# Draining a weight-preparation queue four times as fast inside attention, with its first rounding step moved from VectorE to ScalarE

## The chip, the cores and the metric

The kernel runs on all 8 cores of one Trainium2 chip. Each core takes two of the sixteen sequences (2048 tokens of width 1024) and prepares the FFN weights for itself; the cores do not talk to one another. The time is that of the slowest core, in microseconds (us) of device time. The engines are PE (TensorE), DVE (VectorE), ACT (ScalarE), POOL (GpSimd) and SP (SyncE, here an issuer of transfers). Each has its own instruction stream in program order; semaphores couple them.

## The reference, cut to what matters

Per sequence: attention whose softmax runs over the queries (axis -2), a residual and a layer norm; then an FFN with quantized weights and activations, a depthwise convolution over three tokens, another residual and layer norm.

```python
q, k, v = x @ Wq.T + bq, x @ Wk.T + bk, x @ Wv.T + bv
scores = where(j > i, -inf, q @ k.T / 32)          # [2048, 2048] per sequence
x = layernorm(x + softmax(scores, axis=-2) @ v)

def weight_quant(w):                               # w1: [4096, 1024], w2: [1024, 4096]
    scale = 1.0 / clip(mean(abs(w)), 1e-5)
    return clip(round(w * scale), -1, 1) / scale
h = act_quant(x) @ weight_quant(w1).T
h = silu(depthwise_conv1d(h, conv_w, conv_b))      # 3 taps along the tokens
x = layernorm(x + act_quant(h) @ weight_quant(w2).T)
```

## The kernel before, in words

The program is written as one list of operations (`Prog.op`). Each names its engine and the tiles it reads and writes, and the builder turns dependences into semaphore waits. Within an engine the order is the order of the list. A transfer is issued by the engine that it is listed on, and that engine's stream stands still until the waits of the transfer are met. Transfers on ACT are dealt in turn to four streams (`n_act_dma % 4`), and each also waits for the one before it on its stream; SP's and POOL's wait for the previous one of their engine. A transposing transfer (`xbar=True`) waits for the last transfer of every stream, and all later transfers wait for the last transposing one.

Stages, in order:

- Start (to about 170 us): constants, and Wq, Wk, Wv cast to bf16 into scratch memory.
- `attn(b)` for b = 0 and 1. The x loop (L416 on, 16 tiles) loads x, casts it on DVE, stores it. Then transposing loads of x and Wv (in batch 0 of Wq and Wk too). The v loop (L458 on) has 32 groups of 8 matmuls, each evacuated by DVE (L470). The q and k loops (L476 on) have 32 groups each, evacuated by ACT (L491), over four PSUM banks. The score loop has 16 steps `jt`: matmuls (L521), mask and maxima on DVE (L528, L534), exponentials on ACT (L549), column sums and the scaling of v on DVE (L555 to L561). The PV loop has 16 iterations `it` of 2·(it + 1) matmuls (L578); DVE adds the two banks to x (L585), a layer norm runs over DVE, ACT and POOL, the result is quantized (L636, L640), transposed on PE (L646), copied by ACT (L650) and stored by POOL (L653, s_xqT). At the end of a batch one small store of row maxima (s_m1, L664).
- `ffn_entry()`: 8 transposing loads of the quantized W1 (L815) and 32 of W2. The first waits for all attention tiles and all weight stores.
- The FFN, 16 chunks and a tail.

The weight preparation is a queue of closures, `prep_q`, made by `build_prep_queue()`. It goes over W1 and W2 twice, each in 128 tiles of 128x256. First pass, per matrix: load a tile (`_pload`, L674, issued on ACT), sum its absolute values (`_p1c`, L680, DVE), and at the end one mean (`_pmean`). Second pass: load the tile again, then `_p2c`: three DVE steps (L718: times scale plus MAGIC, which rounds; L723: minus MAGIC, minimum with 1; L727: maximum with -1, to bf16) and a store issued on ACT (L731). Loads are listed three tiles ahead of their compute; there are four input buffers (`PR_in`) and two output buffers (`PR_ob`). The queue has 512 loads, 512 computes and 2 means, 1026 entries. `drain(n)` lists the next n entries at its place; each of the attention loops calls it once an iteration, and `while prep_q: drain(1)` lists what is left between `attn(1)` and `ffn_entry()`.

Of the kernel before, what the change touches and what calls it, by code (L numbers as in the profile page):

```python
# [9 lines left out]
AF = mybir.ActivationFunctionType  # L10
ALU = mybir.AluOpType
AX = mybir.AxisListType.X

MAGIC = 12582912.0
# [166 lines left out]
def build_program(T=2048, NB=2, debug=False):  # L181
# [3 lines left out]
    p = Prog()  # L185
# [65 lines left out]
    misc = P_("misc", [128, 64], F32)  # L251
# [21 lines left out]
    for jt in range(NT):  # L273
# [15 lines left out]
           for t in range(NT)]  # L289
# [18 lines left out]
    PR_in = [mem.at(PRS + i * 1024, f"PR_in{i}", [128, 256], F32)  # L308
             for i in range(4)]
# [44 lines left out]
         writes=["idenf"])  # L354
# [12 lines left out]
    p.op("POOL", lambda e: e.memset(neghalf[:], -0.5), writes=["neghalf"])  # L367
    p.op("POOL", lambda e: e.memset(zpad[:], 0.0), writes=["zpad"])
    p.op("POOL", lambda e: e.memset(misc[:, 60:64], 0.0), writes=["msczero"])

    for b in range(NB):
        for e8 in range(ECH):
# [42 lines left out]
    def attn(b):  # L415
        for it in range(NT):  # L416
            sl = slice(it * 128, (it + 1) * 128)
            p.op("SP", lambda e, sl=sl, it=it: e.dma_start(
                out=A_x32[it % 2][:], in_=x_d[b, sl, :]),
                writes=[f"x32_{it % 2}"], dma=True)  # L420
            p.op("DVE", lambda e, it=it: e.tensor_copy(
                out=A_xbf[it % 2][:], in_=A_x32[it % 2][:]),
                reads=[f"x32_{it % 2}"], writes=[f"xbf{it % 2}"])
            p.op("POOL", lambda e, sl=sl, it=it: e.dma_start(
                out=s_xbf[b, sl, :], in_=A_xbf[it % 2][:]),
                reads=[f"xbf{it % 2}"], writes=[f"sxbf{it}"], dma=True)
            drain(1)
        p.fence([f"xT{e}" for e in range(ECH)]
                + [f"WvT{e}" for e in range(ECH)] + ["BVbc", "bvrow"],
                [f"P{jt}" for jt in range(NT)])  # L430
# [28 lines left out]
        for it in range(NT):  # L459
            g = it % 2  # L460
            bk0, bk1 = 2 * g, 2 * g + 1
            for h, bk in ((0, bk0), (1, bk1)):
                for e8 in range(ECH):
                    p.op("PE", lambda e, it=it, h=h, bk=bk, e8=e8: e.matmul(  # L464
                        out=B[bk][:],
                        lhsT=A_xT[e8][:, it * 128:(it + 1) * 128],
                        rhs=A_WvT[e8][:, h * 512:(h + 1) * 512],
                        start=(e8 == 0), stop=(e8 == ECH - 1)),
                        reads=[f"xT{e8}", f"WvT{e8}"], writes=[f"B{bk}"])
                p.op("DVE", lambda e, it=it, h=h, bk=bk: e.tensor_tensor(  # L470
                    out=A_v[it][:, h * 512:(h + 1) * 512], in0=B[bk][:],
                    in1=A_BVbc[:, h * 512:(h + 1) * 512], op=ALU.add),
                    reads=[f"B{bk}", "BVbc"], writes=[f"v{it}"])
                drain(1)

        icw = min(512, T)  # L476
        for dstl, wTl, bc, nm in ((A_qT, A_WqT, bqc, "q"), (A_kT, A_WkT, bkc, "k")):
            wkey = "WqT" if nm == "q" else "WkT"
            for fc in range(ECH):
                for ic in range(T // icw):  # L480
                    bk = (fc * (T // icw) + ic) % 4
                    for e8 in range(ECH):
                        p.op("PE", lambda e, fc=fc, ic=ic, bk=bk, e8=e8,
                             wTl=wTl: e.matmul(  # L484
                            out=B[bk][:, 0:icw],
                            lhsT=wTl[e8][:, fc * 128:(fc + 1) * 128],
                            rhs=A_xT[e8][:, ic * icw:(ic + 1) * icw],
                            start=(e8 == 0), stop=(e8 == ECH - 1)),
                            reads=[f"xT{e8}", f"{wkey}{e8}"], writes=[f"B{bk}"])
                    p.op("ACT", lambda e, fc=fc, ic=ic, bk=bk, dstl=dstl,  # L490
                         bc=bc: e.activation(  # L491
                        out=dstl[fc][:, ic * icw:(ic + 1) * icw],
                        in_=B[bk][:, 0:icw],
                        func=AF.Identity, bias=bc[:, fc:fc + 1], scale=1.0),
                        reads=[f"B{bk}", "b" + nm + "c"],
                        writes=[f"{nm}T{fc}"])
                    drain(1)

        p.fence([f"P{jt}" for jt in range(NT)],
                [f"xT{e}" for e in range(ECH)] + [f"WvT{e}" for e in range(ECH)]  # L500
# [2 lines left out]
        for jt in range(NT):  # L503
            c0 = jt * 128
            bounds = [c0]
            nxt = (c0 // 512 + 1) * 512
            while nxt < T:
                bounds.append(nxt)
                nxt += 512
            bounds.append(T)  # L510
            chunks = [(bounds[i], bounds[i + 1] - bounds[i])
                      for i in range(len(bounds) - 1)]
            nch = len(chunks)
            banks = []
            for ci in range(nch):
                banks.append(gchunk % 6)
                gchunk += 1
            for e8 in range(ECH):
                for ci, (cs, w) in enumerate(chunks):
                    bk = banks[ci]  # L520
                    p.op("PE", lambda e, e8=e8, jt=jt, cs=cs, w=w, bk=bk: e.matmul(  # L521
                        out=B[bk][:, 0:w],
                        lhsT=A_kT[e8][:, jt * 128:(jt + 1) * 128],
                        rhs=A_qT[e8][:, cs:cs + w],
                        start=(e8 == 0), stop=(e8 == ECH - 1)),
                        reads=[f"kT{e8}", f"qT{e8}"], writes=[f"B{bk}"])
            bk0 = banks[0]
            p.op("DVE", lambda e, bk0=bk0: e.tensor_tensor(  # L528
                out=B[bk0][:, 0:128], in0=B[bk0][:, 0:128], in1=maskneg[:],
                op=ALU.add),  # L530
                reads=[f"B{bk0}", "maskneg"], writes=[f"B{bk0}"])
            for ci, (cs, w) in enumerate(chunks):
                bk = banks[ci]
                p.op("DVE", lambda e, bk=bk, w=w, ci=ci: e.tensor_reduce(  # L534
                    out=misc[:, CMAX0 + ci:CMAX0 + ci + 1], in_=B[bk][:, 0:w],
                    axis=AX, op=ALU.max),
                    reads=[f"B{bk}"], writes=[f"cmax{ci}"])
            p.op("DVE", lambda e, nch=nch: e.tensor_reduce(
                out=mc(MRAW), in_=misc[:, CMAX0:CMAX0 + nch], axis=AX,
                op=ALU.max),  # L540
                reads=[f"cmax{ci}" for ci in range(nch)], writes=["Mraw"])
            p.op("DVE", lambda e: e.tensor_scalar(
                out=mc(BIASV), in0=mc(MRAW), scalar1=-1.0 / 32.0, scalar2=None,
                op0=ALU.mult),
                reads=["Mraw"], writes=["biasv"])
            for ci, (cs, w) in enumerate(chunks):
                bk = banks[ci]
                p.op("ACT", lambda e, bk=bk, w=w, jt=jt, cs=cs, c0=c0,
                     ci=ci: e.activation(  # L549
                    out=A_P[jt][:, cs - c0:cs - c0 + w], in_=B[bk][:, 0:w],  # L550
                    func=AF.Exp, bias=mc(BIASV), scale=1.0 / 32.0,
                    accum_out=misc[:, CSUM0 + ci:CSUM0 + ci + 1]),
                    reads=[f"B{bk}", "biasv"],
                    writes=[f"P{jt}", f"csum{ci}", f"B{bk}_free"])
            p.op("DVE", lambda e, nch=nch: e.tensor_reduce(  # L555
                out=mc(COLSUM), in_=misc[:, CSUM0:CSUM0 + nch], axis=AX,
                op=ALU.add),
                reads=[f"csum{ci}" for ci in range(nch)], writes=["colsum"])
            p.op("DVE", lambda e: e.reciprocal(out=mc(RCOL), in_=mc(COLSUM)),
                 reads=["colsum"], writes=["rcol"])  # L560
            p.op("DVE", lambda e, jt=jt: e.tensor_scalar(  # L561
                out=A_v[jt][:], in0=A_v[jt][:], scalar1=mc(RCOL), scalar2=None,
                op0=ALU.mult),
                reads=["rcol", f"v{jt}"], writes=[f"v{jt}"])
            drain(2)

        p.fence(["xres", "xln0", "xln1", "xqstg", "xqbf", "pvx0", "pvx1"],
                [f"qT{e}" for e in range(ECH)])
        for it in range(NT):
# [73 lines left out]
            for e8 in range(ECH):  # L643
# [11 lines left out]
                .rearrange("e p t -> p e t"),  # L655
                in_=PV_xqstg[:].rearrange("p (e t) -> p e t", e=ECH)),
                reads=["xqstg"], writes=[f"sxq{b}_{it}"], dma=True)
            drain(3)
        p.op("PE", lambda e: e.transpose(
            out=B[5][0:NT, 0:128], in_=m1ct[:], identity=iden_f[:]),  # L660
            reads=["m1ct", "idenf"], writes=["B5"])
# [51 lines left out]
    def _p2c(g, m, sd, rows, cols, skey):  # L713
        rwbk = f"rwb{m + 1}"
        rwbc = RWB1 + m
        up = g % 4
        ob = (g // 1) % 2
        p.op("DVE", lambda e, up=up, rwbc=rwbc: e.tensor_scalar(  # L718
            out=PR_in[up][:], in0=PR_in[up][:],
            scalar1=misc[:, rwbc:rwbc + 1], scalar2=MAGIC,  # L720
            op0=ALU.mult, op1=ALU.add),
            reads=[f"pin{up}", rwbk], writes=[f"pin{up}"])
        p.op("DVE", lambda e, up=up: e.tensor_scalar(  # L723
            out=PR_in[up][:], in0=PR_in[up][:], scalar1=MAGIC, scalar2=1.0,
            op0=ALU.subtract, op1=ALU.min),
# [57 lines left out]
    def drain(n=1):  # L783
        for _ in range(n):
            if prep_q:
                prep_q.pop(0)()
# [391 lines left out]
```

How the kernel before makes its waits and increments, by code:

```python
            def section(_):  # L134
                waited = {f: 0 for f in self.ENGINES}
                for i, emit, inc, deps in ops:
                    want = {}
                    for d in deps:
                        f = openg[d]
                        v = cums[d]
                        if v > want.get(f, 0):
                            want[f] = v
                    for f, v in want.items():
                        if waited[f] < v:
                            eo.wait_ge(sems[f], v)
                            waited[f] = v
                    inst = emit(eo)
                    if inc:
                        inst.then_inc(sems[streams[i]], inc)
```

## Time and profile before

| | us |
|---|---|
| two runs | 3976.15 and 4021.40 |
| their median | 3998.77 |
| the profiled execution | 3978.36 |
| its span on the slowest core (core 3) | 3976.5 |
| spans of the eight cores | 3942.6 to 3976.5 |

| engine | busy us | share of the span |
|---|---|---|
| PE matmul | 2043.1 | 51% |
| DVE | 1608.5 | 40% |
| ACT | 1117.4 | 28% |
| POOL | 153.8 | 4% |

The table of engines is a mean over stages that have different limits. The granted clock of PE is 0.76 of full speed over the span. In the profile's forty slices of 99 us, PE is busy in slices 4 to 17 (attention, in two humps with weak stretches between), at zero in slices 18 to 22, and at seven to eight tenths from slice 24 to the end (the FFN). So a reader looks at stretches of time first, then at what releases what within one.

### The profile page before, as it was taken

The page shows a single profiled execution, that of the slowest core. Times are in us where ns is not written, and L with a number is a line of the kernel's source. Part 1 is how long each engine was busy: PE and PEld are TensorE (multiplying, and loading weights), DVE is VectorE, ACT ScalarE, POOL GpSimd, SP SyncE. Part 2 cuts the span into 40 slices and gives each one's busy share as a digit, 9 for nine tenths or more (in the row PEclk, how much of TensorE's full clock was granted, in tenths as well). Part 3 has the DMA queues.
Part 4 walks back from the last instruction along what each step waited for, and adds up shares of the span by engine and source line. Part 5 has one row for each costly group of instructions (what it writes and reads, how often), then busy time and mean ns, then how long its engine had stood idle before and what let it go on. Part 6 is the DMA issues. An engine that isn't in the chain of part 4 may idle for free.

```text
span 3976.5 us, 43318 instructions; the slowest of 8 cores (3942.6 to 3976.5 us)
## 1 busy us (share of the span) xinstructions
PE 2043.1 (51%) x10824; PEld 1129.4 (28%) x10824; DVE 1608.5 (40%) x4913; ACT 1117.4 (28%) x2978; POOL 153.8 (4%) x264
## 2 busy tenths in 40 slices
PE   0005972341398434300000387777777777787776
PEld 0002430110143111100000254444444444454442
DVE  0102134332122533356650255555555455555554
ACT  0000422220023222100000354444444444444442
POOL 2100000101000010000000000000000000000000
PEclk9998995665598756655555688787888888888877
DMA  1653103224410243355555200000000000000000
GB/s 46 206 137 69 38 19 85 76 81 130 88 38 23 59 86 70 69 148 151 147 139 114 69 17 17 28 27 27 27 27 27 27 25 24 17 27 28 17 22 22
DMA packets 298170, 248.47 MB, mean 62 GB/s; under 512 B 153858, under 2 KB 268738, under 8 KB 297924
## 3 DMA queue, kind: packets, MB, share of 16 engines
q1 hardware_dynamic: 169860, 105.05, 11.1%
q10 hardware_dynamic: 110592, 83.94, 7.7%
q0 software_dynamic: 17472, 56.72, 4.6%
q8 instruction: 92, 1.51, 0.2%
q14 instruction: 154, 1.26, 0.1%
HBM read 138.58 MB, written 73.48 MB: 53 GB/s over the span
## 4 chain that ended last, share of the span: by engine, by line
PE 37%; DMA 23%; DVE 19%; issue 9%; ACT 9%; POOL 1%; DVEq 1%; ACTq 1%; SPq 0%; POOLq 0%
PE bank L993 10%; PE bank L874 8%; PE bank L484 6%; PE bank L578 4%; DVE F_u L981 4%; PE bank L895 3%; DMA s_w2i<-PR_ob 3%; DMA s_w1i<-PR_ob 3%; DVE Fg L984 3%; DMA A_x<-x 3%; DMA F_W2qT<-s_w2i 3%; PE bank L521 3%; PE bank L464 2%; DMA A_xT<-s_xbf 2%; ACT F_D L887 2%
## 5 line engine op out<-in xcount | busy, mean ns | idle before, releaser
L874 PE MATMUL bank<-F_xq,F_W1qT 128*128 128x258 bf16 x4096 | 650.3, 311 | 0.0
L993 PE MATMUL bank<-F_W2qT,Fg 128*128 128x512 bf16 x2048 | 525.5, 395 | 45.3 <-ACT F_ev L1005 39.1
L874 PEld LDWEIGHTS bank<-F_xq,F_W1qT 128*128 128x128 bf16 x4096 | 452.9, 111 | 179.9 <-issue 27.4
L900 ACT ACTIVATE Fg<-bank,cbc 128x256 bf16<-128x256 f32 x512 | 242.7, 474 | 735.8 <-PE bank L895 728.2
L895 PE MATMUL bank<-F_hs,F_D 128*128 128x256 bf16 x1536 | 286.5, 301 | 226.3 <-DVE F_hs L880 111.2
L880 DVE TENSOR_TENSOR F_hs<-bank,F_fbc 128x258 bf16<-128x258 f32 x512 | 217.1, 424 | 335.7 <-PE bank L895 307.1
L862 PE MATMUL bank<-F_fw,ones 1*128 1x258 f32 x32 | 18.6, 680 | 621.5 <-DVE F_fw L858 621.5
L887 ACT ACTIVATE F_D<-iden_f,w0c 128x128 bf16<-128x128 f32 x512 | 201.1, 393 | 409.0 <-DMA s_w2i<-PR_ob 409.0
L993 PEld LDWEIGHTS bank<-F_W2qT,Fg 128*128 128x128 bf16 x2048 | 203.1, 100 | 261.4 <-issue 92.7
L646 PE MATMUL xb<-iden_bf,PV_xqbf 128*128 128x128 bf16 x256 | 63.5, 265 | 408.2 <-DVE PV_xqbf L640 370.8
L895 PEld LDWEIGHTS bank<-F_hs,F_D 128*128 128x128 bf16 x1536 | 144.1, 103 | 313.1 <-issue 289.0
L912 DVE TENSOR_TENSOR F_Mx<-F_Mx,Fg 128x256 bf16<-128x256 bf16 x496 | 143.4, 289 | 205.8 <-ACT Fg L900 201.0
L981 DVE TENSOR_TENSOR F_u<-Fg,F_sbc 128x256 f32<-128x256 bf16 x512 | 214.1, 418 | 0.5
L680 DVE TENSOR_REDUCE PR_ap<-PR_in 128x1 f32<-128x256 f32 x256 | 103.6, 415 | 244.8 <-DMA PR_in<-w 243.8
L464 PE MATMUL bank<-A_WvT,A_xT 128*128 128x512 bf16 x512 | 120.8, 395 | 158.6 <-DMA A_WvT<-s_wv 122.9
L887 ACT ACTIVATE F_D<-iden_f,w1c 128x128 bf16<-128x128 f32 x512 | 200.6, 392 | 0.0
L887 ACT ACTIVATE F_D<-iden_f,w2c 128x128 bf16<-128x128 f32 x512 | 200.5, 392 | 0.0
L578 PE MATMUL bank<-A_v,A_P 128*128 128x512 bf16 x544 | 179.0, 501 | 21.7 <-DVE misc L555 15.8
L862 PEld LDWEIGHTS bank<-F_fw,ones 1*128 1x128 f32 x32 | 7.8, 300 | 625.4 <-issue 625.4
L984 DVE TENSOR_SCALAR Fg<-F_u 128x256 bf16<-128x256 f32 x512 | 150.5, 294 | 56.7 <-DVE F_u L981 3.2
L521 PE MATMUL bank<-A_qT,A_kT 128*128 128x512 bf16 (+3 forms) x640 | 138.7, 374 | 50.2 <-ACT A_P L549 46.7
L646 PEld LDWEIGHTS xb<-iden_bf,PV_xqbf 128*128 128x128 bf16 x256 | 26.5, 104 | 458.4 <-issue 457.7
(126 smaller groups left out, 2121.4 us busy)
## 6 DMA issues: line engine op xcount, KB each, us to landing
PR_in<-w ACTq DMA_DIRECT2D x512, 128.0 KB, 2.4
A_x<-x SPq DMA_DIRECT2D x32, 512.0 KB
PV_xsrc<-x SPq DMA_DIRECT2D x32, 512.0 KB
s_xln<-PV_xln POOLq DMA_DIRECT2D x32, 512.0 KB, 3.0
F_xlnt<-s_xln SPq DMA_DIRECT2D x32, 512.0 KB
out<-F_xlnt POOLq DMA_DIRECT2D x32, 512.0 KB, 3.0
F_xq<-s_xqT SPq DMA_DIRECT2D x128, 64.5 KB
s_xbf<-A_xbf POOLq DMA_DIRECT2D x32, 256.0 KB, 3.2
```

What stands on the lines that cost most here:

```text
L464: p.op("PE", lambda e, it=it, h=h, bk=bk, e8=e8: e.matmul(out=B[bk][:], lhsT=A_xT[e8][:, it * 128:(it + 1) * 128], rhs=A_WvT[e8][:, h * 51 ...
L484: wTl=wTl: e.matmul(out=B[bk][:, 0:icw], lhsT=wTl[e8][:, fc * 128:(fc + 1) * 128], rhs=A_xT[e8][:, ic * icw:(ic + 1) * icw], start=(e8 == ...
L521: p.op("PE", lambda e, e8=e8, jt=jt, cs=cs, w=w, bk=bk: e.matmul(out=B[bk][:, 0:w], lhsT=A_kT[e8][:, jt * 128:(jt + 1) * 128], rhs=A_qT[e8 ...
L578: p.op("PE", lambda e, it=it, jt=jt, h=h, bk=bk: e.matmul(out=B[bk][:], lhsT=A_P[jt][:, it * 128 - jt * 128: it * 128 - jt * 128 + 128], r ...
L874: p.op("PE", lambda e, s=s, e8=e8, bk=bk, par=par: e.matmul(out=B[bk][:, 0:258], lhsT=F_W1qT[e8][:, s * 128:(s + 1) * 128], rhs=F_xq[par][ ...
L880: p.op("DVE", lambda e, s=s, bk=bk, par=par: e.tensor_tensor(out=F_hs[s % 2][:], in0=B[bk][:, 0:258], in1=F_fbc[par][:], op=ALU.mult), rea ...
L887: p.op("ACT", lambda e, k=k, s=s, wc=wc: e.activation(out=F_D[k][s % 2][:], in_=iden_f[:], func=AF.Identity, scale=wc[:, s:s + 1]), reads= ...
L895: p.op("PE", lambda e, k=k, s=s: e.matmul(out=B[2][:, 0:256], lhsT=F_D[k][s % 2][:], rhs=F_hs[s % 2][:, k:k + 256], start=(k == 0), stop=( ...
L900: p.op("ACT", lambda e, s=s, par=par: e.activation(out=F_g[par][s][:], in_=B[2][:, 0:256], func=AF.Silu, bias=cbc[:, s:s + 1], scale=1.0), ...
L981: p.op("DVE", lambda e, cs=cs, par=par, up=up: e.tensor_tensor(out=F_u[up][:], in0=F_g[par][cs][:], in1=F_sbc[:], op=ALU.mult), reads=[f"F ...
L984: p.op("DVE", lambda e, cs=cs, par=par, up=up: e.tensor_scalar(out=F_g[par][cs][:], in0=F_u[up][:], scalar1=MAGIC, scalar2=MAGIC, op0=ALU. ...
L993: p.op("PE", lambda e, par=par, tb=tb, h=h, cs=cs, bk=bk: e.matmul(out=B[bk][:], lhsT=F_g[par][cs][:, tb * 128:(tb + 1) * 128], rhs=F_W2qT ...
```

## The change

The change multiplies each argument of `drain` in attention by four (1, 1, 1, 2, 3 become 4, 4, 4, 8, 12). In `_p2c` it turns the first of the three DVE steps into an ACT activation with the same tile, with the scale from the same column and MAGIC as a bias from a new constant column of `misc`, which one POOL memset fills at the start.

```diff
+    p.op("POOL", lambda e: e.memset(misc[:, 47:48], MAGIC), writes=["magc"])
@@ attn, x loop
-            drain(1)
+            drain(4)
@@ attn, v loop
-                drain(1)
+                drain(4)
@@ attn, q and k loops
-                    drain(1)
+                    drain(4)
@@ attn, score loop
-            drain(2)
+            drain(8)
@@ attn, PV loop
-            drain(3)
+            drain(12)
@@ _p2c
-        p.op("DVE", lambda e, up=up, rwbc=rwbc: e.tensor_scalar(
-            out=PR_in[up][:], in0=PR_in[up][:],
-            scalar1=misc[:, rwbc:rwbc + 1], scalar2=MAGIC,
-            op0=ALU.mult, op1=ALU.add),
-            reads=[f"pin{up}", rwbk], writes=[f"pin{up}"])
+        p.op("ACT", lambda e, up=up, rwbc=rwbc: e.activation(
+            out=PR_in[up][:], in_=PR_in[up][:], func=AF.Identity,
+            scale=misc[:, rwbc:rwbc + 1], bias=misc[:, 47:48]),
+            reads=[f"pin{up}", rwbk, "magc"], writes=[f"pin{up}"])
```

## Rows read from the trace of the kernel before

**Rows 1.** Stretches: us; busy PE, PEld, DVE, ACT, POOL (count); clock, DMA share, GB/s.

```profile
396.00:507.00 111.00, 111.00 (x515) 50.13 (x513) 13.80 (x33) 45.21 (x65) 0.00 (x0) 1.00 0.13 39
...
1070.00:1126.00 56.00, 55.94 (x250) 25.01 (x251) 26.65 (x47) 0.00 (x0) 0.00 (x0) 0.96 0.12 36
...
1680.00:2076.00 396.00, 0.74 (x4) 0.61 (x4) 242.64 (x832) 0.00 (x0) 0.00 (x0) 0.50 0.54 146
```

**Rows 2.** Chain that ended last: start us, length us, what.

```profile
361.61 34.27 PE bank L464 x152
...
666.32 3.43 PE bank L578 x8
...
908.65 9.55 PE bank L578 x32
...
943.60 3.50 DMA s_m<-mrow
...
1643.22 9.20 PE bank L578 x32
...
1671.73 7.46 DMA PR_in<-w
...
2075.99 6.99 DMA F_W1qT<-s_w1i
```

**Rows 3.** Stretch of 31 us, L680 alone: DVE busy (count), clock, DMA share, GB/s.

```profile
1700.00:1731.00 31.00, 14.49 (x36) 0.50 0.59 152
```

**Rows 4.** Tile PR_in: ns min/median/max, first and last start; its loads' landing.

```profile
L718 DVE TENSOR_SCALAR PR_in<-PR_in,misc x256: 345/347/354, 1733.0 to 2073.0; 128x256 f32<-128x256 f32 x128
...
DMA to landing us min/median/max: 2.0/2.4/9.5
```

**Rows 5.** Order of time, score steps 1 and 11 of batch 0: start, length, engine, line.

```profile
525.43 0.30 DVE L528 TENSOR_TENSOR bank<-bank,maskneg 128x128 f32<-128x128 f32 x1 [3.88 <-PE bank L521]
...
602.76 0.20 ACT L549 ACTIVATION_READ_ACCUMULATOR A_P<-bank,misc 128x1 f32 x1
603.06 0.15 DVE L555 TENSOR_REDUCE misc<-misc 128x1 f32<-128x2 f32 x1 [1.53 <-ACT A_P L549]
...
604.32 0.29 DVE L528 TENSOR_TENSOR bank<-bank,maskneg 128x128 f32<-128x128 f32 x1
```

**Rows 6.** Order of time, one second-pass unit in the stage between attention and FFN.

```profile
1747.40 0.29 DVE L723 TENSOR_SCALAR PR_in<-PR_in 128x256 f32<-128x256 f32 x1
1747.87 0.29 DVE L727 TENSOR_SCALAR PR_ob<-PR_in 128x256 bf16<-128x256 f32 x1 [0.17 <-DVE PR_in L723]
...
1748.24 0.35 ACTq L731 DMA_DIRECT2D s_w1i<-PR_ob  x1
...
1748.68 0.39 ACTq L674 DMA_DIRECT2D PR_in<-w  x1
```

**Rows 7.** Groups by line and shape, ACT: busy us, mean ns; idle before.

```profile
L614 ACT ACTIVATE PV_xln<-PV_xres,misc 128x1024 f32<-128x1024 f32 x32 | 39.8, 1243 | 55.4 <-DVE misc L611 55.4
...
L549 ACT ACTIVATE A_P<-bank,misc 128x512 bf16<-128x512 f32 x56 | 38.6, 689 | 52.1 <-DVE misc L542 42.0 <-DMA PR_in<-w 3.7 <-PE bank L521 0.4
...
L549 ACT ACTIVATE A_P<-bank,misc 128x128 bf16<-128x128 f32 x8 | 3.0, 369 | 35.0 <-DVE misc L542 35.0
```

**Rows 8.** Chain, x loads in batch 0's x loop.

```profile
192.05 4.21 DMA A_x<-x
196.38 3.42 DMA A_x<-x
199.86 4.45 DMA A_x<-x
```

**Rows 9.** Order of time, PV iteration 10 of batch 0.

```profile
797.87 3.08 ACT L650 COPY PV_xqstg<-xb 128x128 bf16<-128x128 bf16 x8 [4.44 <-PE xb L646]
...
800.34 7.03 PE L578 MATMUL bank<-A_v,A_P 128*128 128x512 bf16 x22
...
807.54 0.69 DVE L585 TENSOR_TENSOR PV_xres<-bank,PV_xsrc 128x512 f32<-128x512 f32 x1 [1.75 <-PE bank L578]
```

## The prediction

> **What bounds the kernel now.** I read three views: the stretches (how long each stage is, which engine works in it), the chain that ended last, and the order of time inside one unit of the weight preparation. The preparation queue holds 1026 entries: 512 loads, 512 computes, two means. Before, attention drains 16 + 32 + 64 + 16·2 + 16·3 = 192 per batch, 384 in all, so 642 are left for a stage of their own between attention and FFN. The reader sees it in [rows 1], last line: 396 us with PE, ACT and POOL idle and DVE 61% busy, all of it ended by the transposes of W1 that wait for the last store [rows 2]. The FFN stage behind is the same program before and after; I carry it over unchanged.
>
> **What goes.** In batch 0 the last 32 PV matmuls start at 908.65 and the m1 store that closes the batch ends at 947.10: 38.45 us. Batch 1's last 32 start at 1643.22, so without a queue left the W1 transposes could start at about 1681.7 instead of 2075.99 [rows 2]: **-394 us**. The new quotas are 64 + 128 + 256 + 128 + 192 = 768 per batch, so the queue ends in batch 1's q loop, 66 entries in. Behind it, batch 1 has no reductions between its steps any more: 12 score steps by 0.33 us: **-4**. The one added memset is on idle POOL before anything reads it: 0.
>
> **The price of a unit.** First-pass unit (load, reduce; 256 of them): 36 in 31 us, 0.86 us each, when nothing else runs [rows 3]. Second-pass unit (load, three elementwise steps, store; 256): before, L718 starts 256 times between 1733.0 and 2073.0 [rows 4], 1.33 us each. The change puts its first step on ACT. ACT also issues that unit's store, which waits for DVE's last step, then a load, and only then can take the next unit's first step: ACT and DVE must alternate. The cycle, from rows: step on ACT 0.60; ACT to DVE 0.10 (the accumulator read ends at 602.96, DVE starts at 603.06 [rows 5]); DVE's two steps start 0.47 apart; store issued 0.37 after the second one starts; load 0.44 after the store; next ACT step about as long after the load's issue, 0.42 [rows 6]. Sum **2.40 us**, against 1.33. The ACT step is not in the trace. Nearest rows: L614 is the same form (Identity, column scale and bias, SBUF f32 to SBUF f32) at 1024 columns, 1243 ns; L549 grows by (689 - 369)/384 = 0.833 ns a column; 1243 - 768·0.833 = 603 ns [rows 7]. Bounds: L549's line would give 689 - 256·0.833 = 476 ns for 256 columns, giving a cycle of 2.27; a slower handover on ACT (0.55 for 0.42) gives 2.55. L718 on DVE took 347 ns [rows 4]. The Trainium skill, "ScalarE: Activation LUTs", section "Rules for kernel authors", tells to keep multiply and add on VectorE; the rows agree (347 against about 603), and by the rule alone the edit would cost the ACT-DVE difference, 256·0.26 = 66 us at most; the sum here goes by the alternation instead.
>
> **Who pays in attention.** Stage by stage, with P1 for the first pass and P2 for the second:
>
> - Batch 0, x loop (P1, two units a tile instead of half): an x load takes 3.42 alone and 4.21 or 4.45 when a 128 KB preparation load runs beside it [rows 8]: 0.9 each on average. Tile 3.42 + 1.8 = 5.2 against about 3.9, the mean of the two kinds: 16·1.3 = **+21**.
> - Batch 0, v loop: loads drained there wait for the last weight transpose (the xbar order), and a compute behind them blocks DVE. At one entry a group PE got 13 groups done before 361 us; at four, computes run out in the third group, and with four banks PE does 7. 25 groups are then left instead of 19 (152 matmuls in 34.3 us [rows 2]). Two units want 1.72 us [rows 3], a PE group 1.73 (111/64 [rows 1]); interlocked I take 1.85: 46 - 35 = **+11** (0 to 50).
> - Batch 0, q and k: 64·(1.85 - 1.73) = **+8**. Here ACT does 0.69 of evacuation (512 columns, [rows 7]) and two issues, which fits.
> - Batch 0, scores. Steps 0 to 3: DVE waits 3.9 us for PE anyway [rows 5], 0. Steps 4 to 7: four units, the fourth's load issued when the exps end: 2.4 landing [rows 4] + 0.35 + 0.42 = 3.2 against 1.36 (602.96 to 604.32 [rows 5]): 4·1.8 = +7. Step 8 has the second mean, five short DVE steps and two matmuls in series, and a load that nothing fetched ahead (2.4 again); I estimate +9. Steps 9 to 15: DVE is free about 1.0 after the exps (three short steps), its two steps of the first unit take 0.76, then three cycles of 2.4, so the next mask step comes at 9.0, not 1.36: 7·7.6 = +53. Together **+69**.
> - Batch 0, PV: six units behind the copies. Copies end at 800.95; the last DVE step of the sixth unit is done 5·2.40 + 1.46 = 13.5 later (1.46 = 0.60 + 0.10 + 0.47 + 0.29 for the last unit's own steps); the second bank's add then 0.8 after that, 14.2 after the copies. Before, it started at 807.54, 6.6 after, which is PE's 7.03 less 0.44 [rows 9]. So an iteration pays 14.6 less its PE time. PE's times run from 3.43 (it 3) to 9.55 (it 15) [rows 2]; 13 such rows and two small ones I estimate (1.7, 2.6) sum to 85.5: 15·14.6 - 85.5 = 134, and 3 for the burst behind the last, which POOL's store of s_xqT mostly covers: **+137**.
> - The same bursts run while that store of s_xqT is on its way. A preparation load beside it took 7.46 us to chain on [rows 2], against the median 2.4 and a longest of 9.5 [rows 4]; the load issued first in a burst is needed 5.2 us on. That is 2.3 late, and stores, which free a buffer every second unit, may be late too: I take 2.5·15 = **+37** (0 to 75).
> - Batch 1, x loop: per tile two loads and two stores of half the size: 3.42 + 2·(0.9 + 0.45) = 6.1, more than two cycles (4.8): 16·2.2 = **+35**.
> - Batch 1, v loop: two cycles a group, 32·4.8 = 154 against 56 [rows 1]: **+98**. DVE's add fits in its gaps.
> - Batch 1, q loop: 16.5 groups of 4.8 + 0.6 (the evacuation stands in ACT's chain) against 1.73: **+61**.
>
> Sum of costs 477; 477 - 394 - 4 = +79. The profiled execution took 3978.4 us (span 3976.5 and 2 around it), which is near the faster of the two runs and 20 below their median of 3998.8. 3978 + 79 = **4057 us**.
>
> **Rivals.** *A, the alternation does not bite (faster, 0.12).* If ACT ran the next unit's step while DVE does this one's, a unit would keep about 1.33. The exposed cycles are 7·3 in scores, 15·5 in PV, 64 and 33 in batch 1's v and q, 193 in all: 193·1.07 = 206 less, **3851 us**. For it: ACT is only 28% busy and the step itself is short. Against: the store's issue sits before the next step in ACT's order and follows DVE's last step by 0.37 in the tail [rows 6]. It decides the sign once the cycle is below 2.0. The Trainium skill, "Perfetto Trace Analysis", section "Per-instruction lifecycle" (on the DMA instruction), has the sequencer itself wait for a DMA's semaphores, so nothing behind it starts; the rows agree.
>
> *B, the ends meet further up (slower, 0.24).* Stores and loads beside the s_xqT store reach 7.5 us each time, so a burst loses 5 (+75 instead of 37), and x tiles in both batches cost half as much again (+28): 3978 + 79 + 38 + 28 = **4123 us**. For it: the 7.46 of [rows 2]. Against: the median of 2.4 [rows 4]. It decides against no change once the overlap costs 25 us more than I took.
>
> *C, the PE clock (slower, 0.12).* If PE, now waiting a little in every v, q and k group of batch 0, is granted 1.2 GHz (0.50 in the profile, as in the last line of [rows 1]) a group takes twice 1.73 us: 89 groups by 3.46 - 1.85 is +143 if it stays there, **4200**; half the time, 4129. Against: PE then has no idle time left, and after long idle stretches the trace has it back at 0.96 and 1.00 in the v and q loops [rows 1].
>
> *D, the change does nothing*, 642 entries still left: excluded by the quotas, 1536 against 1026.
>
> **How the numbers follow.** My case (4057, its own range 4015 to 4095 from the cycle bounds, 193·(-0.13 to +0.15), and the spread of the overlap terms) has 0.52. A difference of about 2% is what a measurement of this kernel can tell from none. My case lies near that bound, which is 4079 from the median before and 4058 from the profiled execution, so I split it nearly in two: 0.41 within 2% and 0.11 slower. B and C, 0.36, are slower. A, 0.12, is faster. Range 3950 to 4150: it leaves out most of A and C's far end, 0.2 in all. Chances: faster 0.12, within 2% 0.41, slower 0.47.
>
> **What would show it.** A stage between attention and FFN gone (W1 transposes right behind the last m1 store), the new ACT step at about 0.60 us, starts of that step 2.4 us apart in bursts (rival A: 1.3 to 1.5), batch 1's v groups 4.8 us apart, PV iterations of batch 0 that no longer grow with `it`, q and k of batch 0 still near 111 us at clock 1.00 (rival C: 0.5 to 0.8). Wrong would be: an FFN much off its 1741 us (2235 to the end of the span), or a cycle off 2.40 by over 0.3.

## The result, and the profile after

The changed kernel takes 4012.05 us in the median (19 runs, 4004.95 to 4041.13) against 3981.21 us before (18 runs, 3969.49 to 4035.03). The ratio is 1.0087, with a 95% interval of 1.0065 to 1.0108. The change is slower by a little under one per cent: a 396 us stage went away, and attention grew by more. The direction and the places were as forecast, but the forecast surplus of 79 us came out as 31 in the medians and 37 in the spans of the two profiled executions (3976.5 and 4013.1 us). The sum had several terms that were too dear. In some executions, whatever the kernel, one die runs late at a lower clock; where they move a median below, the time without them stands beside it.

First the chain that ended last in the changed kernel (start us, length us, what). It holds the borders of the stages; from the added memset to `_p2c` the lines are one higher than before.

```profile
247.79 5.65 DMA A_xT<-s_xbf
...
375.07 46.27 PE bank L465 x200
...
421.35 13.83 PE bank L485 x64
...
534.80 6.43 PE bank L522 x29
...
1198.63 4.46 DMA s_m<-mrow
...
1282.99 4.78 DMA A_xT<-s_xbf
...
1343.83 3.36 DMA A_WvT<-s_wv
...
1679.56 6.43 PE bank L522 x29
...
2079.80 9.22 PE bank L579 x32
...
2112.25 6.84 DMA F_W1qT<-s_w1i
```

The W1 transposes now stand 32.45 us behind the start of batch 1's last 32 PV matmuls; in [rows 2] the distance was 432.8. The x200 in the second line are the 25 v groups that the prediction counted. The same borders in the kernel before (its own chain: 240.48, 361.61, 395.88, 507.32, 947.10, 1007.19, 1070.06, 1238.69, 1643.22, 2075.99) give the ledger:

| stretch | before | after | measured change | predicted |
|---|---|---|---|---|
| start to the first x transpose, batch 0 | 240.5 | 247.8 | +7.3 | +21 |
| transposes to the long v run | 121.1 | 127.3 | +6.2 | 0 |
| rest of v | 34.3 | 46.3 | +12.0 | +11 |
| q and k | 111.4 | 113.5 | +2.0 | +8 |
| scores and PV, batch 0 | 439.8 | 668.3 | +228.5 | +243 |
| x loop, batch 1 | 60.1 | 79.9 | +19.8 | +35 |
| transposes | 62.9 | 64.2 | +1.3 | 0 |
| v, q, k, batch 1 | 168.6 | 332.4 | +163.7 | +159 |
| scores and PV, batch 1 | 404.5 | 400.2 | -4.3 | -4 |
| last PV matmuls to the W1 transposes | 432.8 | 32.5 | -400.3 | -394 |
| from there to the end | 1900.5 | 1900.8 | +0.3 | 0 |

The two chains are of two cores, core 3 before and core 7 after. The medians of all eight cores agree with the table within 5 us in all rows but one: scores and PV of batch 0 take 441.0 and 665.1 us (+224), batch 1's x loop 60.5 and 79.4 (+19), its v, q and k 169.9 and 332.7 (+163), the last stretch to the W1 transposes 429 and 33 (-396). The exception is "transposes to the long v run". Measured from the first x transpose to the end of the last one of Wk, it is 114.8 before and 113.4 after in the median; core 7 is the slowest of the eight there, with 120.9. The +6.2 is that core's and not the change's. The median span grows from 3970.1 to 3997.2 us, by 27.

Inside batch 1's v loop the order of time shows the alternation. These are start, length and instruction of one unit and the start of the next:

```profile
1441.53 0.60 ACT L719 ACTIVATE PR_in<-PR_in,misc 128x256 f32<-128x256 f32 x1 [1.83 <-DVE A_v L471]
1442.23 0.29 DVE L723 TENSOR_SCALAR PR_in<-PR_in 128x256 f32<-128x256 f32 x1 [1.06 <-ACT PR_in L719]
1442.70 0.29 DVE L727 TENSOR_SCALAR PR_ob<-PR_in 128x256 bf16<-128x256 f32 x1 [0.17 <-DVE PR_in L723]
...
1443.08 0.35 ACTq L731 DMA_DIRECT2D s_w2i<-PR_ob  x1
1443.51 0.40 ACTq L675 DMA_DIRECT2D PR_in<-w  x1
1443.96 0.60 ACT L719 ACTIVATE PR_in<-PR_in,misc 128x256 f32<-128x256 f32 x1 [1.82 <-DVE PR_ob L727]
```

The step takes 0.60 us (603 ns estimated), DVE starts 0.10 behind its end, its second step 0.47 later, the store 0.38 after that, the load 0.43 later, and the next step 0.45 after the load (0.42 taken). Together 2.43 us against the 2.40 of the sum. ACT was idle 1.82 us before its step, until DVE had finished with the unit before.

A PV iteration of batch 0 pays at the end of its burst of six units. In time order:

```profile
942.51 0.60 ACT L719 ACTIVATE PR_in<-PR_in,misc 128x256 f32<-128x256 f32 x1
...
945.45 0.60 ACT L719 ACTIVATE PR_in<-PR_in,misc 128x256 f32<-128x256 f32 x1 [2.33 <-issue]
...
949.58 0.29 DVE L727 TENSOR_SCALAR PR_ob<-PR_in 128x256 bf16<-128x256 f32 x1 [0.65 <-DMA s_w1i<-PR_ob]
...
956.84 0.29 DVE L727 TENSOR_SCALAR PR_ob<-PR_in 128x256 bf16<-128x256 f32 x1 [0.17 <-DVE PR_in L723]
957.05 0.68 DVE L586 TENSOR_TENSOR PV_xres<-bank,PV_xsrc 128x512 f32<-128x512 f32 x1
```

PE had finished this iteration's 14 matmuls by 949; DVE takes up their result at 957.05, because the sixth unit's last step stands before it in DVE's order. Two disturbances are in the burst: the first unit takes 2.94 us, the third's last step waits for a store. From the first ACT step to 957.13 it is 14.6 us. Over all 120 such bursts of the eight cores the median is 14.8 us, and in this kernel the results of successive iterations are taken up every 30 us whatever `it` is, where it was 16 us early and 24 late in the loop before.

### The profile page after: what moved, and what is told of

The parts are those of the page before. It is cut to its first block, busy times and chain, and to the rows that moved or that the text cites. A ratio compares the mean times of both kernels' runs of the same rounds, so it can differ in the third digit from the quotient of the medians.

```text
span 4013.1 us, 43031 instructions; the slowest of 8 cores (3989.7 to 4013.1 us)
## 1 busy us (share of the span) xinstructions
PE 2106.8 (52%) x10824; PEld 1138.2 (28%) x10824; DVE 1538.1 (38%) x4657; ACT 1261.5 (31%) x3234; POOL 153.7 (4%) x265
## 4 chain that ended last, share of the span: by engine, by line
PE 32%; DVE 21%; DMA 18%; ACT 12%; issue 11%; ACTq 4%; DVEq 1%; POOL 1%; POOLq 0%; SPq 0%
PE bank L993 10%; PE bank L874 8%; PE bank L485 4%; DVE F_u L981 4%; ACT PR_in L719 3%; PE bank L895 3%; DVE Fg L984 3%; DMA F_W2qT<-s_w2i 3%; PE bank L522 2%; PE bank L579 2%; DMA s_w1i<-PR_ob 2%; ACTq L675 2%; DMA A_xT<-s_xbf 2%; ACT F_D L887 2%; DVE PR_ob L727 2%
## 5 line engine op out<-in xcount | busy, mean ns | idle before, releaser
L719 ACT ACTIVATE PR_in<-PR_in,misc 128x256 f32<-128x256 f32 x256 | 153.3, 599 | 492.6 <-issue 206.4
L465 PE MATMUL bank<-A_WvT,A_xT 128*128 128x512 bf16 x512 | 147.2, 447 | 236.6 <-DMA A_WvT<-s_wv 132.5
L723 DVE TENSOR_SCALAR PR_in<-PR_in 128x256 f32<-128x256 f32 x256 | 75.6, 295 | 446.1 <-ACT PR_in L719 446.1
```

The lines of the kernel that those rows point to most:

```text
L719: p.op("ACT", lambda e, up=up, rwbc=rwbc: e.activation(out=PR_in[up][:], in_=PR_in[up][:], func=AF.Identity, scale=misc[:, rwbc:rwbc + 1], ...
```

## Experiments

The theory: the quotas save about 400 us and cost little where a unit is cheap; the step moved to ACT makes the unit of the second pass dear (2.43 us for 1.33), since on ACT the next unit's step is listed behind a store and a load that wait for DVE. The rivals: the units are bound by their transfers; or the 0.60 us of the ACT step itself is the price, whatever the order.

### The quotas alone

```diff
# the changed kernel, with the first step back on DVE
-        p.op("ACT", lambda e, up=up, rwbc=rwbc: e.activation(
-            out=PR_in[up][:], in_=PR_in[up][:], func=AF.Identity,
+        p.op("DVE", lambda e, up=up, rwbc=rwbc: e.tensor_scalar(
+            out=PR_in[up][:], in0=PR_in[up][:],
```

> Only the quotas of the change; the first step of a second-pass unit stays on DVE. My theory: the quotas take the stage between attention and FFN away (-394 us, as recorded) and the second-pass unit in bursts keeps about its old cadence of 1.33 us, because ACT then holds only issues and nothing in its order waits for DVE and is waited for by DVE. About 193 cadences are exposed in attention, so against the changed kernel (4012 us) 193 x (2.43 - 1.33) = 212 us less: 3800 us. Rival: the units in attention are limited by their transfers, not by the alternation of ACT and DVE; then the cadence stays at 2.2 us or more and the time at 3970 or above.

Measured: 3789.77 us, ratio to the kernel before 0.9543 (0.9497 to 0.9590). So the quotas alone make it 4.6% faster, and the changed kernel's 222 us above it belong to the step. In batch 1's v loop, in DVE's order of time:

```profile
1310.41 0.35 DVE L718 TENSOR_SCALAR PR_in<-PR_in,misc 128x256 f32<-128x256 f32 x1
...
1312.07 0.34 DVE L718 TENSOR_SCALAR PR_in<-PR_in,misc 128x256 f32<-128x256 f32 x1
...
1313.20 0.35 DVE L718 TENSOR_SCALAR PR_in<-PR_in,misc 128x256 f32<-128x256 f32 x1
...
1314.93 0.34 DVE L718 TENSOR_SCALAR PR_in<-PR_in,misc 128x256 f32<-128x256 f32 x1
```

From 1312.07 to 1314.93 are two units and one evacuation of v: 2.86 us, where the changed kernel takes 4.9. The transfers are the same in both, so they do not set the 2.43 there.

In PV the rival is partly right. A burst of six units at 1.33 us would take about 8 us; it takes 11.5 in the median, because with two output buffers DVE's last step waits for the store of two units before:

```profile
919.24 0.29 DVE L727 TENSOR_SCALAR PR_ob<-PR_in 128x256 bf16<-128x256 f32 x1 [4.22 <-DMA s_w1i<-PR_ob]
```

That is still 3.3 us less than the 14.8 of the changed kernel. The burst also starts sooner: its first step is no longer listed on ACT behind the eight copies, through which DVE stood idle for 4.4 us before its first step of the burst (L723) in the changed kernel. So in PV the step on ACT costs by both, its alternation and its place behind the copies; no run separates the two. Scores and PV of batch 0 take 553 us in the median of the cores, 112 less than in the changed kernel, and batch 1's v, q and k 218, 115 less.

### The step alone

```diff
# the kernel before, with the change's memset and its first step on ACT; quotas 1, 1, 1, 2, 3
```

> Only the move of the first step to ACT; quotas as before, so 256 units run in a stage with nothing else beside them. My theory: cycle 2.43 us as read in the changed kernel's trace, instead of 1.33: 256 x 1.10 = +282 us, 4263 us. Rival (the alternation is a matter of the crowded attention stage, an idle stage hides it): a unit at 1.4 to 1.6 us, 4000 to 4050 us.

Measured: 4260.32 us, ratio 1.0737 (1.0659 to 1.0814). The instructions of the step (ns min/median/max, first and last start), and three units in order of time:

```profile
L719 ACT ACTIVATE PR_in<-PR_in,misc x256: 599/599/601, 1785.5 to 2402.4; 128x256 f32<-128x256 f32 x128
```

```profile
1899.83 0.60 ACT L719 ACTIVATE PR_in<-PR_in,misc 128x256 f32<-128x256 f32 x1 [1.83 <-DVE PR_ob L727]
...
1902.19 0.60 ACT L719 ACTIVATE PR_in<-PR_in,misc 128x256 f32<-128x256 f32 x1 [1.76 <-DVE PR_ob L727]
...
1904.62 0.60 ACT L719 ACTIVATE PR_in<-PR_in,misc 128x256 f32<-128x256 f32 x1 [1.83 <-DVE PR_ob L727]
```

255 cycles in 616.9 us are 2.42 each; in [rows 4] they were 1.33. Nothing else runs in this stage, so neither the crowd in attention nor other work on ACT makes the cycle. By the medians this step costs 284 us alone and 222 beside the quotas (4012 against 3790), as in attention part of the cycles lies under other work.

### The step kept, the order loosened

```diff
-    PR_in = [... for i in range(4)]
+    PR_in = [... for i in range(5)]        # and up = g % 5
@@ _p2c: the ACT step of this unit, then the store of the unit before
         p.op("ACT", lambda e, up=up, rwbc=rwbc: e.activation(...))
+        while late:
+            late.pop(0)()
...
-        p.op("ACT", lambda e, ...: e.dma_start(out=sd[rows, cols], in_=PR_ob[ob][:]), ...)
+        late.append(lambda ...: p.op("ACT", lambda e: e.dma_start(...), ...))
```

> The changed kernel with a fifth input buffer, and each unit's store listed behind the next unit's ACT step, so that nothing on ACT between two ACT steps waits for the DVE steps of the unit just handed over. The ACT step itself stays. My theory: the cycle falls to ACT's own work, 0.60 for the step and 0.44 + 0.44 for two issues, with a small gap 1.5 to 1.65 us instead of 2.43; 193 x 0.85 = 164 us less than 4012: 3850 us. Rival (it is the landing of loads and stores that sets the cycle): no lower than 2.2 us, 3970 us or more. Second rival (the 0.60 us of the ACT step is the cost, not the order): hardly any change from 4012.

Measured: 3874.70 us in the median of 5 runs; the two with both dies alike took 3832.61 and 3834.68, and these, the profiled one among them, are compared here. ACT's order in batch 1's v loop:

```profile
1303.31 0.60 ACT L720 ACTIVATE PR_in<-PR_in,misc 128x256 f32<-128x256 f32 x1 [0.61 <-DVE PR_in L726]
...
1304.51 0.60 ACT L720 ACTIVATE PR_in<-PR_in,misc 128x256 f32<-128x256 f32 x1 [0.60 <-DVE PR_in L726]
...
1305.74 0.60 ACT L720 ACTIVATE PR_in<-PR_in,misc 128x256 f32<-128x256 f32 x1 [0.62 <-DVE PR_in L726]
```

The same ACT step of 0.60 us comes every 1.2 us in these rows, and every 1.4 in the mean of batch 1's v loop (2.46 in the changed kernel), quicker than the 1.5 to 1.65 expected. The store's issue starts 0.32 us after the step, at 1303.63, while the step is still running; the load's issue follows 0.44 later and the next step 0.44 after that. Some 178 us are gone with the step still on ACT, so the second rival (its duration) falls as well. Batch 1's v, q and k take 222 us, nearly the 218 of the kernel with the step on DVE. In scores and PV of batch 0 only about half comes back: 606 us, against 665 and 553. There the ACT steps still stand behind the copies, and the output buffers wait for their stores:

```profile
902.11 0.29 DVE L730 TENSOR_SCALAR PR_ob<-PR_in 128x256 bf16<-128x256 f32 x1 [4.07 <-DMA s_w1i<-PR_ob]
```

This kernel has two edits, the fifth buffer and the place of the store. No run separates them.

### The store of s_xqT behind the burst

```diff
+            drain(12)
             p.op("POOL", lambda e, it=it: e.dma_start(out=s_xqT[...], in_=PV_xqstg[...]),
-                reads=["xqstg"], writes=[f"sxq{b}_{it}"], dma=True)
-            drain(12)
+                reads=["xqstg"], writes=[f"sxq{b}_{it}"], dma=True,
+                deps=[last DVE op listed] if it < NT - 1 else ())
```

> The changed kernel, but in each PV iteration except a batch's last the store of s_xqT waits for the last DVE step of the preparation burst, so the two no longer run side by side. The trace of the changed kernel has a burst of six units at 14.7 us from the first ACT step to the last DVE step (942.5 to 957.1), against 5 x 2.43 + 1.46 = 13.6 for undisturbed cycles: 1.1 us an iteration. Theory now: 15 x 1.1 = 17 us less than 4012, 3995 us, and the burst at 13.6. The recorded prediction priced this overlap at 37 us, which would give 3975. Rival: the overlap costs nothing, 4012, and the burst stays at 14.7.

Measured: 3997.68 us, ratio to the kernel before 1.0026 (0.9985 to 1.0067), where the changed kernel has 1.0087. By the ratios it is 0.6% or about 24 us, and the two intervals just overlap; but six of the twelve executions lie between 3987 and 3989 us, below the lowest of the changed kernel's (4004.95), and the trace carries the reading. A burst of six units in time order:

```profile
956.02 0.60 ACT L721 ACTIVATE PR_in<-PR_in,misc 128x256 f32<-128x256 f32 x1
...
969.17 0.29 DVE L729 TENSOR_SCALAR PR_ob<-PR_in 128x256 bf16<-128x256 f32 x1 [0.17 <-DVE PR_in L725]
969.38 0.68 DVE L586 TENSOR_TENSOR PV_xres<-bank,PV_xsrc 128x512 f32<-128x512 f32 x1
```

It takes 13.4 us from the first step to the end of the last, against 14.6 in the changed kernel: 1.2 us for each of 15 iterations, 18 us. It is not one burst's luck: over 120 bursts of the eight cores the medians are 13.6 and 14.8 us, and scores and PV of batch 0 take 646.9 us against 665.1, 18.2 less. The recorded prediction had put 37 on it.

### The x loops, empty and doubled

```diff
# the quotas alone (first step on DVE), and in both x loops
-            drain(4)
+            drain(0)     # first kernel
+            drain(8)     # second kernel
```

> Quotas of the change with the first step on DVE, but no entries at all in the two x loops; read is the time per tile there, not the total. The recorded prediction took 3.42 us for a tile without transfers beside it, and 0.9 for each 128 KB load beside it, which makes 55 us for an x loop of 16 tiles. Rival: the tile is set by the serial chain of x load, cast and store with its own mean of 3.75 us, and the alternation of 3.4 and 4.4 us seen before was not a price per load: then an empty loop takes 3.7 us a tile as well, about 60 us between the m1 store and the first x transpose in batch 1.

> The same with 8 entries a tile in both x loops. Batch 0: four 128 KB loads a tile. By the recorded price 3.42 + 4 x 0.9 = 7.0 us a tile. By the price read from the changed kernel (4.5 us at two loads, 3.75 at half a load: 0.5 each) 5.5 us. Batch 1: four loads and four stores a tile; recorded price 8.8 us; by cadence, 4 x 1.33 plus the cast 0.7 = 6.0 us.

The profiled execution of the empty kernel took 3751.08 us (three runs, median 3784.95), the only run of the doubled one 3827.38. What was asked is the time of the loop. The first x transpose of batch 0 started, in the chain of the empty and then of the doubled kernel:

```profile
235.71 4.99 DMA A_xT<-s_xbf
```

```profile
254.79 4.66 DMA A_xT<-s_xbf
```

With half a load a tile it was 240.48 (before), with two 247.79 (after). These are single cores, and the cores start the loop up to 6 us apart. So take for each core the time from its first x load to its first x transpose, and of the eight cores the median (one execution of each kernel):

| loads a tile | batch 0, us | spread of the cores | over empty, per load and tile |
|---|---|---|---|
| 0 (empty) | 64.6 | 64.1 to 65.5 | |
| half (before) | 69.2 | 68.1 to 70.4 | 0.58 |
| 2 (changed kernel) | 77.5 | 76.2 to 78.5 | 0.41 |
| 4 (doubled) | 87.9 | 84.7 to 90.2 | 0.37 |

None of these is 0.9. The chain shows why one price per load is the wrong form. Before, it goes over the x loads [rows 8]; in the changed kernel it goes over the stores of x in bf16, with 0.5 us between the landing of one and the start of the next:

```profile
205.05 3.70 DMA s_xbf<-A_xbf
...
209.30 3.72 DMA s_xbf<-A_xbf
...
213.56 4.62 DMA s_xbf<-A_xbf
```

In the doubled kernel it goes over the preparation's own loads. The rivals written before the runs come out: 3.77 us for an empty tile (60.4/16 in batch 1) where 3.7 was written, and 5.5 for four loads (87.9/16) where 5.5 was written and 7.0 recorded.

In batch 1 the loop, from the m1 store to the first x transpose, takes 60.4 us empty and 60.5 before: no price for that half load. With the new quotas its units are of the second pass, with a store each. With two units a tile it takes 74.5 with the step on DVE and 79.4 in the changed kernel. Doubled it takes 127.6, that is 8.0 us a tile: neither the 8.8 of the recorded price nor the 6.0 of the cadence. There the chain holds one store of prepared weights a tile, and DVE stands idle for 51 us of the loop until such stores have landed:

```profile
1133.01 4.96 DMA s_w2i<-PR_ob
...
1141.30 4.66 DMA s_w2i<-PR_ob
...
1149.77 4.51 DMA s_w2i<-PR_ob
```

So the units' transfers do get dear where DVE waits for a store to free one of the two output buffers, and the cadence alone missed that. The stretches of the x loop in batch 0 (busy time by engine, then clock, DMA share, GB/s), of the empty kernel, the changed one and the doubled one:

```profile
172.00:235.00 63.00, 3.75 (x4) 1.17 (x4) 12.74 (x19) 0.00 (x0) 9.71 (x18) 1.00 0.64 208
```

```profile
174.00:247.00 73.00, 3.75 (x4) 1.16 (x4) 21.75 (x48) 0.00 (x0) 9.42 (x17) 1.00 0.74 223
```

```profile
174.00:254.00 80.00, 3.75 (x4) 1.16 (x4) 34.42 (x78) 0.00 (x0) 9.02 (x16) 1.00 0.84 253
```

The DMA engines moved 208 GB/s at a share of 0.64 with x alone, and 253 at 0.84 with four more loads a tile. The x loop is two chains side by side, of loads and of stores, each with one transfer on its way at a time, and leaves room beside it. The recorded price was built on the difference between two kinds of tile ([rows 8]), as if each load added it again.

### Quotas placed where an engine waits

```diff
# first step on DVE, and
-            drain(4)                       # x loop
+            drain(4 if b == 0 else 3)
-                drain(4)                   # v loop; the same in q and k
+                drain(4 if b == 0 else 2)
-            drain(8)                       # scores
+            drain(8 if jt < 4 else 2)
-            drain(12)                      # PV
+            drain(2 * (2 + it // 3))
```

> A version meant to beat both: first step on DVE, quotas placed where an engine waits anyway. Batch 0: 4 entries in x, v, q and k loops (first-pass units there cost next to nothing: q and k took 113.5 us in the changed kernel against 111.4 before). Scores: 8 in the first four steps, where DVE waits for PE, then 2. PV: 4 entries at the start growing to 14 at the end with the matmul time that hides them. Batch 1: 3 in the x loop, 2 in v, q and k, where one unit of 1.33 us fits under a group of 1.73. My theory: -394 from the stage, about +75 in attention: 3660 us. If placement does not matter (only the number of entries does), it comes out as the kernel with the quotas alone, 3800 us.

Measured: 3671.98 us, ratio 0.9238 (0.9176 to 0.9300): faster than both kernels, by 7.6% against the one before. Borders in its chain:

```profile
532.13 6.43 PE bank L521 x29
...
984.26 3.97 DMA s_m<-mrow
...
1123.05 56.06 PE bank L464 x249
...
1290.60 6.43 PE bank L521 x29
...
1745.78 6.03 DMA F_W1qT<-s_w1i
```

Scores and PV of batch 0 take 456.1 us (439.8 before, 668.3 in the changed kernel). Batch 1's v, q and k take 167.6 us, with 96 units in them, against 168.6 before and 332.4 in the changed kernel. The stretch itself:

```profile
1123.00:1290.00 167.00, 166.95 (x764) 75.28 (x764) 101.53 (x320) 43.54 (x64) 0.00 (x0) 0.99 0.40 113
```

PE is busy for 166.95 of 167 us, and DVE does 101.5 us of work beneath: one unit fits under a group of 1.73 us, so it costs nothing there. It is not free everywhere: in the median of the cores batch 1's x loop takes 71.7 us (60.5 before) and its scores and PV 424.6 (403.6 before). Of the 309 us below the kernel before, 191 are there with the quotas alone; 118 come from the placement.

## Why the prediction was right and wrong

**Right.** *The price of a unit*: 2.40 forecast, 2.43 in attention, 2.42 alone; the ACT step 603 ns forecast, 599 measured. The reading of the order on ACT was the cause: the loosened order takes nearly all of the price back in batch 1's v, q and k and half of it in scores and PV, with the step in place. *What goes*: 394 forecast, 400 measured; in the end stretch the s_xqT store no longer has preparation loads beside it, which is likely the other 6, though no run isolates it. *Batch 1's v and q*: 159 against 163.7. *Scores and PV of batch 0 without the overlap*: 69 + 137 = 206 forecast; with the s_xqT store moved away they take 646.9 - 441.0 = 205.9 more than before. *Batch 0's v*: 11 against 12. *The -4 in batch 1*: -4.3. The FFN was unchanged, within 0.3 us in the two chains. Rivals A and C did not come: the cycle is as long as feared, and q and k of batch 0 ran at clock 1.00 in 113.5 us. Rival B was the wrong way round: the overlaps cost less than taken, not more.

**Wrong: the size of the terms that stand for transfers beside transfers.** Of 79 us predicted, 42 did not come in the two profiled spans, and 48 by the medians of the runs.

- "Batch 0, x loop", "0.9 each on average", and "Batch 1, x loop", 6.1 us a tile. The step that failed is the addition of one price per load. Measured are 7.3 and 19.8 us for 21 and 35, together 29 too much. The runs with 0 and 8 entries show 0.58, 0.41 and 0.37 us per load in batch 0 as loads are added, on a tile of 3.77 us and not 3.42. In batch 1 two units a tile cost 4.66 us a tile (74.5/16) when the step is on DVE, and 4.96 in the changed kernel, near two cycles of 2.43; its chain there goes over the steps and issues of the units. So the alternation set the pace, and the transfers alone would have set one a little below. The sum also took 3.9 us for this tile before, where the ledger has 60.1/16 = 3.76.
- "The same bursts run while that store of s_xqT is on its way", +37 by 2.5 us an iteration. It was 1.2 us, about 18. The term took the longest landing in view (7.46 us) for a usual one. That accounts for the 14.5 us by which scores and PV of batch 0 fell short.
- "q and k", +8 for an interlock of 1.85 us a group: 2.0 measured. Two units of 0.86 us fit under 1.73 almost wholly.

So the case itself was right and its place near the 2% bound was not. The 0.47 for slower by over 2% rested on those terms, on B and on C. With 27, 18 and 2 us for these three in place of 56, 37 and 8, the 79 would have been 25; the measured 31 and 37 hold further differences of up to 6 us a row with both signs, the +6.2 of core 7 among them.

## What to carry to other kernels

Before a step is moved to an engine that also issues the transfers of the same loop, write out that engine's order for two turns: a transfer that waits for the other engine holds back the next turn's step, and the cost is what the round trip adds (here 1.1 us a unit), not the difference of two durations (0.25). One more buffer and a store listed one turn later, tried together, undo it where that engine has little else to do; where it has copies of its own, half the cost stayed. And background work belongs where an engine waits, in portions no longer than the wait: the same 1026 entries cost 31 us with equal factors and the alternation, and gave back over 300 us with the cheap unit when placed by the profile, 118 of them by the placement.

## What the runs showed of the hardware that I had not expected

A 128 KB load beside the x transfers of batch 0 costs less per load as more are added: 0.58, 0.41, 0.37 us each at half, two and four loads a tile, while the traffic rises from 208 (none) to 253 GB/s (four). A DMA share of 0.64 was no ceiling. With stores beside them it is otherwise: four loads and four stores a tile brought the tile from 3.8 to 8.0 us. And on ACT the issue of a transfer can run under an activation: with no wait between them, a store's issue starts 0.32 us after the start of a step of 0.60, and step, store issue and load issue repeat every 1.2 us.
